# Attention on one core: four float32 groups a unit instead of six, and single products behind score pairs

## What is computed

```python
xt = jnp.transpose(x, (0, 2, 1))
qh = (xt @ Wq.T).reshape(B, T, 8, 32).transpose(0, 2, 1, 3)
scores = scale * jnp.einsum('bhqd,bhkd->bhqk', qh, qh)
logits = (scores * cmask + (1.0 - cmask) * NEG) * rmask
ctx = jnp.einsum('bhqk,bhkd->bhqd', jax.nn.softmax(logits, axis=-1), qh)
out = jnp.transpose(ctx.transpose(0, 2, 1, 3).reshape(B, T, D) @ Wo.T, (0, 2, 1))
```

## Time and profile before

| | us |
|---|---|
| median of 3 runs (lowest, highest) | 1970.55 (1961.05, 1976.32) |
| the profiled execution | 1962.56 |
| its span in the trace | 1960.8 |
| TensorE busy in the span | 1861.1 |
| VectorE busy | 978.1 |
| ScalarE busy | 734.7 |
| GpSimd busy | 663.6 |

### The profile page before, as it was taken

How to read it: one execution, slowest core, us unless ns; L and a number is a source line. 1 busy time by engine, 2 the same in 40 slices (tenths; PEclk the granted TensorE clock), 3 DMA queues, 4 the chain that set the end, 5 groups by cost and what they waited for, 6 DMA issues and landing times. The chain is left out here.

```text
span 1960.8 us, 27850 instructions
## 1 busy us (share of the span) xinstructions
PE 1861.1 (95%) x9512; PEld 1384.4 (71%) x9513; DVE 978.1 (50%) x1605; ACT 734.7 (37%) x1432; POOL 663.6 (34%) x500
## 2 busy tenths in 40 slices
PE   4999999999999769899999999999999999999999
PEld 2545555555554357798898999878788888888887
DVE  3777777777778258432333332254523333333333
ACT  1567777776776522343344443331001010101000
POOL 3577777777775526111111111111100101010100
PEclk9799999999999979899999999989999999999999
DMA  7767767776874073632333322262502121211111
GB/s 135 105 110 125 121 97 134 122 115 113 125 105 61 22 238 96 202 105 95 119 120 119 116 83 76 75 193 75 193 22 87 33 75 35 72 43 64 43 44 43
DMA packets 117636, 193.89 MB, mean 99 GB/s; under 512 B 11856, under 2 KB 43600, under 8 KB 117552
## 3 DMA queue, kind: packets, MB, share of 16 engines
q1 hardware_dynamic: 106912, 157.93, 36.2%
q0 software_dynamic: 10640, 34.87, 6.1%
HBM read 99.40 MB, written 42.21 MB: 72 GB/s over the span
## 5 line engine op out<-in xcount | busy, mean ns | idle before, releaser
L387 DVE TENSOR_REDUCE maxcol<-ps_m 128x1 f32<-128x512 f32 x512 | 330.3, 686 | 164.3 <-PE ps_m L550 161.5
L326 ACT ACTIVATE e<-ps_e 128x512 f32<-128x512 f32 x512 | 288.6, 599 | 168.6 <-PE ps_e L545 167.2
L1437 ACT ACTIVATE s_silu<-s_ps_g 128x512 f32<-128x512 f32 x77 | 46.0, 597 | 556.2 <-PE s_ps_g L1560 556.2
L1405 POOL DMA_INDIRECT s_chosen<-routed,s_slot_now x64 | 63.4, 991 | 563.5 <-DVE s_total L1491 552.9
L1516 DVE TENSOR_TENSOR s_h_f<-s_silu,s_ps_u 128x512 f32<-128x512 f32 x77 | 53.0, 688 | 391.0 <-PE s_ps_u L1560 365.8
L135 POOL TENSOR_TENSOR e<-e 128x2048 f32<-128x2048 f32 x64 | 224.6, 3510 | 69.1 <-ACT e L326 69.1
L545 PE MATMUL ps_e<-qside,kside 98*128 98x512 f32 x512 | 223.1, 440 | 7.1 <-DMA qside<-maxrow 5.1
L550 PE MATMUL ps_m<-kside,qside 97*128 97x512 f32 x512 | 213.8, 422 | 14.9 <-DMA qside<-row_mask 12.3
L545 PEld LDWEIGHTS ps_e<-qside,kside 98*128 98x128 f32 x512 | 97.2, 191 | 122.2 <-ACT e L326 81.0
L1075 DVE TENSOR_TENSOR e_h_lo<-e_ps_h,e_h_hi 128x256 fp32r<-128x256 f32 (+1 forms) x136 | 41.9, 350 | 222.4 <-ACT e_h_hi L890 222.4
L1572 PE MATMUL s_ps_y<-s_d_hi,s_h_hi 128*128 128x512 f32 x352 | 137.9, 392 | 1.1 <-DVE s_h_lo L1473 0.6
(11 more groups left out here) (241 smaller groups left out, 3914.1 us busy)
## 6 DMA issues: line engine op xcount, KB each, us to landing
routed<-keep_y SPq DMA_DIRECT2D x68, 256.0 KB, 2.0
kside<-q_hi SPq DMA_DIRECT2D x64, 256.0 KB
qside<-qm_hi SPq DMA_DIRECT2D x64, 256.0 KB
x_f<-in_x SPq DMA_DIRECT2D x16, 512.0 KB, 4.1
kside<-q_lo SPq DMA_DIRECT2D x32, 256.0 KB
qside<-qm_lo SPq DMA_DIRECT2D x32, 256.0 KB
attn<-xo SPq DMA_DIRECT2D x32, 256.0 KB, 2.5
keep_rows<-attn SPq DMA_DIRECT2D x8, 1024.0 KB, 5.7
```

Source lines behind the costliest of these rows:

```text
L326: act.activation(e[kb][:, g, :], ps_e[g % 2][:, :], ACT.Exp, scale=SCALE).then_inc(e_done, 1)
L387: dve.reduce_max(maxcol[par][:, g * KB + kb:g * KB + kb + 1], ps_m[g % 2][:, :], AX.X).then_inc(max_done, 1)
L1405: pool.indirect_dma_start(out=chosen[k][s % 2][:], out_offset=None, in_=routed, in_offset=bass.IndirectOffsetOnAxis(ap=slot_now[:, k, s:s ...
```

## The change

TensorE: the second denominators now stand behind the numerators in the group of (1,1), the values ahead of the numerators of (3,1), and the first denominators behind these; so four groups are left. The logits of a batch go to the head of the group of (0,1), one unit later. Projection and output products stand one or two at a time behind score pairs, as three tables say. The last product of an output half stands in the next unit. PSUM: maxima and logits use ps_q, the partial logits ps_den, so ps_o holds only output and transposed rows. VectorE: its half of pair 1 stands behind (0,1), the inverses two at a time behind (2,1) and (3,1), and the copy of the logits goes to ScalarE. GpSimd: the low part of x stands last, behind the masked q. ScalarE: the copies are spread anew. SP: the store follows the new place of the output half. The diff, cut:

```diff
+    INVERT = {(2, 1): (0, 1), (3, 1): (2, 3)}
+    PROJECT = {(0, 3): (0,), (1, 0): (1, 2), (1, 2): (3,), (1, 3): (4,), (2, 0): (5,)}
+    OUT = {(2, 2): (0,), (2, 3): (1,), (3, 0): (2,), (3, 2): (3,), (3, 3): (4,)}
+    OUT_NEXT = {(0, 0): (5,)}
+    def gated(u):
+        return (u - 6) // 2 if u % 2 == 0 else -1
...
-            half, b = 1 - n % 2, (u - 4 + n % 2) // 2
-            if 0 <= b < NB:
+            half, b, _ = batches(u)
+            if a_batch(b):
                 upto(sp, o_done, KT * b + half + 1)
...
-            if n % 2 == 1 and known(i, n, 5):
...
-                pool.tensor_tensor(x_lo[:], x_f[bp][:], x_hi[:], ALU.subtract).then_inc(x_split, 1)
             if known(i, n):
                 add_pair(pool, u, 0, slice(0, HG), pair_pool)
...
                 pool.tensor_tensor(qm_lo[par][:], q_lo[par][:], mask_b[bp][:], ALU.mult).then_inc(q_split, 1)
+            if n % 2 == 1 and known(i, n, 5):
...
+                pool.tensor_tensor(x_lo[:], x_f[bp][:], x_hi[:], ALU.subtract).then_inc(x_split, 1)
...
             for kb in range(KB):
-                if kb == 1 and known(i, n, -1):
-                    copy_numerators(i, n)
                 if kb == 2 and known(i, n, -1):
                     copy_denominators(i, n)
                 for g in range(HG):
                     if known(i, n):
                         weights(i, n, kb, g)
+                    if (kb, g) == (0, 1):
+                        if a_batch(gated(RING * i + n)):
+                            copy_logits(i, n, gated(RING * i + n))
+                        if known(i, n, 1):
+                            copy_maxima(i, n)
+                        if a_batch(turned):
+                            copy_out_rows(turned, odd)
+                    if (kb, g) == (0, 2) and known(i, n, -1):
+                        copy_numerators(i, n)
+                    if (kb, g) == (1, 1) and known(i, n, -2):
                         context_high(i, n)
+                    if (kb, g) == (1, 2) and a_batch(turned):
                         copy_turned_rows(turned, odd)
+                    if kb == 2 and 1 <= g <= 2 and known(i, n, 4):
+                        copy_q(i, n, g - 1)
                     if (kb, g) == (2, 2) and odd and a_batch(turned):
                         copy_partial(turned)
+                    if (kb, g) == (3, 1):
+                        if odd and known(i, n, 5):
+                            x_high(i, n)
+                        if known(i, n, 4):
+                            copy_values(i, n)
...
-                    if g == 1 and kb == 1 and known(i, n, -1):
+                    if g == 1 and kb == 0 and known(i, n, -1):
                         add_pair(dve, u - 1, 1, slice(0, HG // 2), pair_dve)
-                    if g % 2 == 1 and kb >= 2 and known(i, n, -1):
+                    if (kb, g) in INVERT and known(i, n, -1):
                         dve.wait_ge(den_done, u)
-                        dve.reciprocal(den[par][:, c], den[par][:, c]).then_inc(over_done, 1)
+                        for at in INVERT[kb, g]:
+                            c = slice(at * T // PARTS, (at + 1) * T // PARTS)
+                            dve.reciprocal(den[par][:, c], den[par][:, c]).then_inc(over_done, 1)
...
         def fp32_group(i, n, kb, before):
+            if kb == 0 and a_batch(gated(u)):
+                logits(u, gated(u))
             if kb == 0 and known(i, n, 1):
                 turn_maxima(i, n)
+            if kb == 3 and known(i, n, 4):
+                turn_values(i, n)
             if before:
                 numerators(*before)
+            if kb == 1 and known(i, n, -1):
+                denominators(u - 1, 1)
             if kb == 1 and a_batch(turned):
                 turn_rows(u, turned, odd)
             if kb == 2 and odd and a_batch(turned):
+                partial_logits(u, turned)
+            if kb == 3 and known(i, n):
+                denominators(u, 0)
...
-                    if g == 3 and kb == 0 and known(i, n, 4):
-                        project(i, n)
+                    if known(i, n, 4):
+                        for m in PROJECT.get((kb, g), ()):
+                            project(i, n, m)
+                    if a_batch(projected):
+                        for m in OUT.get((kb, g), ()):
+                            out_rows(u, projected, 1 - odd, m)
+                    if a_batch(batches(u - 1)[2]):
+                        for m in OUT_NEXT.get((kb, g), ()):
+                            out_rows(u - 1, batches(u - 1)[2], odd, m)
                     if g == 1:
                         fp32_group(i, n, kb, before)
-                    if g == 3 and kb == 2 and a_batch(projected):
-                        out_rows(u, projected, 1 - odd)
-                    if g == 3 and kb == 1:
-                        if known(i, n, -1):
-                            denominators(u - 1, 1)
-                        if known(i, n, 4):
-                            turn_values(i, n)
-                    if g == 3 and kb == 3:
-                        if known(i, n):
-                            denominators(u, 0)
-                        if odd and a_batch(turned):
-                            logits(u, turned)
```

More of the change, by code:

```diff
@@ L25, in attention @@
     PARTS = 4
+    INVERT = {(2, 1): (0, 1), (3, 1): (2, 3)}
+    PROJECT = {(0, 3): (0,), (1, 0): (1, 2), (1, 2): (3,), (1, 3): (4,), (2, 0): (5,)}
+    OUT = {(2, 2): (0,), (2, 3): (1,), (3, 0): (2,), (3, 2): (3,), (3, 3): (4,)}
+    OUT_NEXT = {(0, 0): (5,)}
+    TERMS = 3 * KT
     def sb(name, shape, dt):
@@ L273, in copy_maxima, with copy_logits @@
                 act.wait_ge(maxrow_in[(n - 1) % RING], 16 * (i + (n - 1) // RING + 1))
-            act.activation(maxrow[(n + 1) % 2][:, :], ps_o[0:HG * KB, 0:P], ACT.Copy, scale=-1.0).then_inc(mt_done, 1)
+            act.activation(maxrow[(n + 1) % 2][:, :], ps_q[0:HG * KB, 0:P], ACT.Copy, scale=-1.0).then_inc(mt_done, 1)
+        def copy_logits(i, n, b):
+            act.wait_ge(lg_mm, b + 1)
+            if known(i, n, 1):
+                act.wait_ge(mt_mm, RING * i + n + 2)
+            act.activation(keep["logits"][:, KT * b:KT * (b + 1), :],
+                           ps_q[:, P:P + KT * NE].rearrange("p (h e) -> p h e", h=KT), ACT.Copy).then_inc(lg_done, 1)
         def copy_values(i, n):
@@ L309, in copy_partial @@
             upto(act, lg_mm, b)
-            act.activation(partial[:], ps_o[:, 0:KT * P], ACT.Copy).then_inc(partial_done, 1)
+            act.activation(partial[:], ps_den[:, 0:KT * P], ACT.Copy).then_inc(partial_done, 1)
         def x_high(i, n):
@@ L406, in _, with part @@
         pe.wait_ge(setup, 3)
[L408 to L413, removed]
+        def part(out, a, b, m):
+            t, term = m // 3, m % 3
+            l, r = ((a[0], b[0]), (a[0], b[1]), (a[1], b[0]))[term]
+            return nc.tensor.matmul(out, l(t), r(t), start=(m == 0), stop=(m == TERMS - 1))
         def numerators(u, n, kb):
@@ L431, in denominators @@
                 upto(pe, den_done, u)
+                odd, turned, _ = batches(u)
+                if odd and a_batch(turned):
+                    pe.wait_ge(partial_done, turned + 1)
             if pair == 1:
@@ L478, in turn_rows, with partial_logits @@
             last.then_inc(xt_mm, 1)
-        def partial_logits(b):
+        def partial_logits(u, b):
             pe.wait_ge(xt_done, KT * (b + 1))
+            upto(pe, den_done, min(u, NU))
             for k in range(KB):
-                last = nc.tensor.matmul(ps_o[k * P // KB:(k + 1) * P // KB, 0:KT * P], gate_w[:, k, :], xo_t[:, k, :], start=True, stop=True)
+                last = nc.tensor.matmul(ps_den[k * P // KB:(k + 1) * P // KB, 0:KT * P], gate_w[:, k, :], xo_t[:, k, :], start=True, stop=True)
             last.then_inc(partial_mm, 1)
@@ L522, in fp32_group @@
             if kb == 2 and odd and a_batch(turned):
-                partial_logits(turned)
+                partial_logits(u, turned)
+            if kb == 3 and known(i, n):
+                denominators(u, 0)
         def step(i, n):
```

89 lines of the change are left out of this document (34 added, 55 removed).

## The result

Timed in turns with the kernel before on one chip, 20 runs each, the changed kernel takes 1976.23 us (median) against 1963.93: ratio 1.0061, 95% interval 1.0048 to 1.0074. One of its 20 executions took 3032.82 us at a mean granted clock of 0.559, where the others had 0.97 to 0.98, and is not in the ratio. The forecast was 1980.0 and "no change, on the slow side". The profiled execution of the changed kernel took 1980.25 us (span 1978.4).

A forecast was written before the change was run, and what follows sets the result against it. TensorE's order was taken to bound attention. Terms -1.1, -0.64, +0.5, +0.3, +1.9 gave +0.9 to 1.0 us a pair, +11 over 12 pairs, ends -1: +10 on the 1970.6 median, forecast 1980 us, range 1955 to 1998.

The forecast's parts named there:

- Two groups fewer: TensorE's merged groups: fewer entry and exit steps, less a cost for value transposes; minus 1.1 us a pair of units.
- The wait of the output half: TensorE before the odd unit's output products: the idle time for the partial logits' copy goes, minus 0.64 us a pair.
- Two reciprocals in a row: VectorE behind (2,1): paired inverses delay the maxima, so TensorE waits before m(3,0) in even units; plus 0.5 us.
- ScalarE, +0.3: Odd units: the partial logits' copy stands ahead of exp (2,3), for which e(3,1) waits; plus 0.3 us.
- VectorE's sum, +1.9: Moved behind (0,1), it and GpSimd block each other; TensorE waits before m(1,0), 1.25 odd, 0.65 even; plus 1.9 a pair.
- Transfers: Start of attention: earlier x stack saves 3 to 5 us of waiting, set against losses of units 1 to 3: nothing.
- The end: Last units of the attention: ScalarE alone sets the pace there, a win of about 1 us.
- the sums miss each other: Rival on the VectorE and GpSimd pair sums: no blocking cost, the 1.9 a pair falls away; 1957 us, chance 0.22.
- everything is covered: Rival: reciprocals, ScalarE copy and sum all cost nothing, some 4 us of start gain kept; 1944 us, chance 0.08.
- The even unit tips: Rival: GpSimd's product ends before 1.96, its long sum goes first, VectorE's starts later; some +15, 1995 us, chance 0.20.
- fifth step: VectorE's half of the pair sum moves to where GpSimd works and is blocked; plus 1.9 us a pair.
- first: The step on TensorE's two removed groups; minus 1.1 us a pair, bounds 0.8 and 1.3.

The follow-up runs named there:

- one input: Changed kernel with VectorE's half of the pair sum replaced by a maximum over the same columns, result unused: 1948.84 us, ratio 0.9922 to the kernel before.
- GpSimd alone in odd units: Changed kernel with GpSimd adding all four heads of pair 1 in odd units, even units unchanged: 1958.74 us, ratio 0.9976 to the kernel before.
- the later copy: Changed kernel with ScalarE's copy of the partial logits in odd units moved from ahead of exp(2,3) to ahead of exp(3,0): 1973.17 us, ratio 1.0044.
- combined: Changed kernel, GpSimd alone adding pair 1 in odd units, VectorE's half at (0,0) in even, first two output reciprocals apart, partial copy at (3,0): 1949.73 us, ratio 0.9927.

## Why the prediction was right, step by step

Its steps, a pair of units each, against the rows above (pair 39.12 from 311.18 to the same point 350.30, where the earlier trace rows have 38.27: +0.85 for a forecast of +0.9 to 1.0; over all 12 pairs it is +0.74, 8.8 us for a forecast of 11, since some pairs of the kernel before wait for the row of maxima and take more than 38.27):

- **Two groups fewer, -1.1.** Not seen by itself; what is left of 39.12 without the waits (1.74, 0.42, 0.33) is 36.63, against 38.27 less 0.64: -1.0. Numerators to denominators are 0.88 as taken, the value transposes 0.53 (306.10 to 306.63) for 0.59.
- **The wait of the output half, -0.64.** Gone.
- **Two reciprocals in a row, +0.5.** The wait is 0.17 by the bracket and 0.42 by the starts (0.32 and 0.1 behind it). They take 1.75 for 1.64: 0.82 is the spacing behind a first one, which takes 0.94, and the prediction left that out.
- **ScalarE, +0.3.** e(3,1) in the odd unit is 0.23 late and 0.1 more behind it; moving the copy gave 0.43.
- **VectorE's sum, +1.9.** 1.19 and 0.55, for 1.25 and 0.65. Both chains hold in time: in the odd unit I had GpSimd's sum over at 3.3 and VectorE's at 4.4 after the unit's start; with the start at 310.01 they ended at 3.37 and 4.44. In the even unit (start 329.87) GpSimd's product was to end at 3.0 and did at 3.06. One reading was off: in the earlier trace rows VectorE is done at 669.96 and GpSimd at 668.88, 1.08 apart and not 1.22. The run with one input and the one with GpSimd alone in odd units show that this is the step that decides; with an unblocked VectorE the changed kernel, its denominators incomplete, is 15 us faster than the kernel before.
- **Transfers.** Wrong in the netting: the 3 to 5 us gain was there (5.1), the losses of units 1 to 3 set against it were not. The end was wrong in sign: -1 forecast, +3.7 found. TensorE's waits from 600 to 720 us that grew, of the changed kernel and then of the kernel before:

```profile
PE ps_e L567 <- ACT e L343: 3.7, 8, 0.5
PE ps_den L454 <- POOL e L144: 2.6, 2, 2.5
```

```profile
PE ps_e L545 <- ACT e L326: 1.8, 2, 1.3
PE ps_den L436 <- DVE e L135: 1.1, 1, 1.1
```

  The last units have no projection products to space their pairs, so eight short waits for ScalarE took the place of two; other waits there shrank (for the turned rows), and all together they grew by only 1 us. The clock falls in the same 10 us in both kernels (0.89 and 0.88 from 670 to 680), while the changed one is some 6 us further back (its last numerators end at 674.47, those of the kernel before at 668.33), so more of it runs at the lower level. I take that for the rest; no run tests it.

The total was 10 for 12.3 found, on a base that stood 6.6 us above the median of the runs made later. The steady state is where the prediction was right by its mechanism. That the total came so near is luck in part: start and end were -5.1 and +3.7 for 0 and -1, and cancel; the profiles show +7.4 for the attention, and the 4.9 from there to the 12.3 of the medians rest on the one profile of the kernel before, which no run tests; and the base was too high by more than the change was too small. Of the rivals, "the sums miss each other" fell by the 2162 ns; "everything is covered" by the 18.4 us of waits. "The even unit tips" did not come about: x_lo ended at 1.83 (1.85 forecast), and the run with the later copy shows how near it is: 0.3 us in ScalarE's order changes who goes first, there to the better.

What the prediction did not see is that its fifth step was bound to its first. It priced the move as if the quiet place had been free to keep; the run with the sum at (1,1) shows that it costs 1.8 us a pair there as well. It also gave no price to the clock behind a wait, which was right for this change (1.00 throughout) but by a small margin.

## What to carry to other kernels

Before moving an elementwise operation with two SBUF inputs on VectorE, write down what GpSimd executes in that stretch: its end, not the operation's start, sets when the result is there. Giving the whole operation to the "slower" engine can be faster than sharing it. When a group of products is moved earlier, look at what feeds it, since the feeding step may lose its only quiet place; and price a wait of TensorE with the lower clock that may follow it.

## What was unexpected of the hardware

- Waits of 1.42 to 1.45 us in a TensorE otherwise busy without a break were followed by the lower clock in five of 12 cases in one kernel, and waits of 1.75 to 1.80 in all 11 of another; waits of up to 1.3 us (combined) between 140 and 600 us never were, in any run. The fall costs about 1.7 us, as much again as such a wait.
- A blocked VectorE sum ended 1.07 to 1.09 us after GpSimd let go, however long it had taken in all (2.15, 2.46 and 3.19 us in the rows above; 29 sums in the changed kernel): of the 1.22 us that it takes alone, no more than some 0.14 is done while it is blocked.
- Reciprocals on VectorE, which read one tile in SBUF and write it back, took 0.89 to 0.95 us whether GpSimd worked or not.
